# Heads ordered by weight norms, first squares beside the casts, one store per part of Q and K, operand rows loaded ahead of the shift row, last four projections inside the score loop

## The reference

```python
q = (xn @ Wq) * mod; k = (xn @ Wk) * mod; v = (xn @ Wv) * mod     # mod: cos(phase) * amplitude, per head and dim
scores = einsum('bhid,bhjd->bhij', q, k) / sqrt(D)
scores = scores * cos(2 pi (i - j) / S)
w = softmax(scores); w = (w + roll(w, 1)) / sqrt(2)
attn = einsum('bhij,bhjd->bhid', w, v) @ Wo
# experts: 8 logits per token from xn @ wqkv.T, top 2, softmax over the two
ffn = sum over the two experts e: score * ((silu(a) * g) @ w2[e].T), with a, g = split(xn @ w1[e].T)
out = x + attn + ffn
```

## Time and profile before

| | us |
|---|---|
| median of 3 runs | 681.27 (680.93 to 682.08) |
| the profiled execution's own time | 681.02 |
| its span | 679.1 |
| first score matmul starts | 49.67 |
| PE busy in the span | 595.2 (88%) |
| ACT busy in the span | 524.2 (77%) |

### The profile page before, as it was taken

How to read it: one execution, slowest core, us unless ns; L and a number is a source line. 1 busy time by engine, 2 the same in 40 slices (tenths; PEclk the granted TensorE clock), 3 DMA queues, 4 the chain that set the end, 5 groups by cost and what they waited for, 6 DMA issues and landing times.

```text
span 679.1 us, 11462 instructions
## 1 busy us (share of the span) xinstructions
PE 595.2 (88%) x4181; PEld 209.4 (31%) x4181; DVE 199.2 (29%) x491; ACT 524.2 (77%) x489; POOL 81.7 (12%) x94
## 2 busy tenths in 40 slices
PE   2887766389999999999999999999999998888985
PEld 1341111013333334333333333333333331211213
DVE  6675511002123232323333232332323220000233
ACT  2649945398888788887887888888878889999992
POOL 4100176500000000000000000000000003455000
PEclk9997787599999999999999999999999999999999
DMA  8345122404322224132131322223222100111002
GB/s 236 117 131 171 42 65 67 134 22 130 115 77 82 84 76 117 52 106 68 58 117 60 100 75 84 82 60 99 83 77 82 44 9 21 36 33 34 9 1 65
DMA packets 42813, 52.99 MB, mean 78 GB/s; under 512 B 7245, under 2 KB 32359, under 8 KB 42499
## 3 DMA queue, kind: packets, MB, share of 16 engines
q1 hardware_dynamic: 39616, 47.71, 23.4%
q0 software_dynamic: 2048, 4.20, 2.1%
q10 hardware_dynamic: 1090, 0.30, 0.3%
HBM read 38.54 MB, written 13.63 MB: 77 GB/s over the span
## 4 chain that ended last, share of the span: by engine, by line
PE 58%; ACT 18%; issue 15%; another core or an unknown queue 3%; DVE 2%; DMA 1%; ACTq 1%; SPq 0%; DVEq 0%
PE ps L1270 25%; PE ps L1253 16%; ACT big L652 15%; PE ps L1189 7%; PE ps L1198 5%; ACT cs L644 2%; PE ps L1087 2%; PE ps L1277 1%; PE ps L1287 1%; ACTq L578 1%; PE ps L1179 1%; PE ps L1228 1%; DMA ang<-L_attn_quantum_amplitude 1%; PE ps L1075 1%
## 5 line engine op out<-in xcount | busy, mean ns | idle before, releaser
L652 ACT ACTIVATE big<-ps 128x1536 f32<-128x1536 f32 (+1 forms) x410 | 482.0, 1245 | 114.3 <-PE ps L1253 89.8
L1270 PE MATMUL ps<-big,vh 128*32 128x512 f32 x2048 | 269.5, 616 | 0.0
L1253 PE MATMUL ps<-qa,ka 49*128 49x512 f16 x896 | 164.9, 395 | 52.0 <-ACT big L652 42.0
L1253 PEld LDWEIGHTS ps<-qa,ka 49*128 49x128 f16 x896 | 39.3, 94 | 256.2 <-ACT big L652 221.2
L1189 PE MATMUL ps<-xgT,store 128*128 128x128 f32 (+1 forms) x468 | 72.5, 291 | 0.0
L961 DVE TENSOR_REDUCE m<-ps 128x1 f32<-128x512 f32 x64 | 44.3, 692 | 94.0 <-PE ps L1287 94.0
L1270 PEld LDWEIGHTS ps<-big,vh 128*32 128x32 f32 x2048 | 45.6, 109 | 75.3 <-issue 60.5
L1189 PEld LDWEIGHTS ps<-xgT,store 128*128 128x128 f32 (+1 forms) x468 | 55.7, 181 | 28.2 <-issue 28.2
L532 POOL COPY vh<-vaug 128x144 f32 x16 | 5.1, 319 | 433.8 <-PE ps L1270 407.6
L908 DVE SCALAR_TENSOR_TENSOR cs<-cs,ps 128x384 f32<-128x384 f32 x39 | 21.6, 554 | 75.0 <-ACT cs L644 75.0
L901 DVE COPY xgT<-ps 128x128 f32<-128x128 f32 x39 | 11.4, 292 | 92.0 <-PE ps L1179 92.0
(11 more groups left out here) (164 smaller groups left out, 231.8 us busy)
## 6 DMA issues: line engine op xcount, KB each, us to landing
store<-in_L_ffn_w SPq DMA_DIRECT2D x39, 352.0 KB, 3.0
store<-in_L_ffn_w SPq DMA_DIRECT2D x39, 192.0 KB, 3.1
qk_parts<-store SPq DMA_DIRECT2D x16, 256.0 KB
qa<-qk_parts SPq DMA_DIRECT2D x27, 128.0 KB
slots_x<-vh SPq DMA_DIRECT2D x5, 512.0 KB, 6.2
cs<-slots_x SPq DMA_DIRECT2D x20, 128.0 KB, 3.1
slots_y<-y SPq DMA_DIRECT2D x19, 128.0 KB, 3.1
ka<-qk_parts SPq DMA_DIRECT2D x31, 64.0 KB, 2.2
```

What stands on the lines that cost most here:

```text
L652: nc.scalar.activation(probs[:, prob_of(tiles[0]):prob_of(tiles[-1]) + 1, :], ps[:, bank_of(tiles[0]):bank_of(tiles[-1]) + 1, :], ACT.Exp, ...
L1253: ins = nc.tensor.matmul(ps[:, bank_of(n), :], k[at:at + KQ, P * o:P * o + P], q[at:at + KQ, CW * c:CW * c + CW], start=True, stop=True, t ...
L1270: ins = nc.tensor.matmul(ps[32 * c:32 * c + 32, O_BANKS[p % 2], :], vh[:, p % 2, o + 8 * b, :], probs[:, prob_of(n), :], start=k == 0, sto ...
```

## The change

- `qk_parts` is laid out as [which, part, cos or sin, head, dim, token] instead of [which, head, part, row, token]. A part of a set is stored with one DMA of all 128 partitions (4 DMAs for the first two sets instead of 8, and 4 instead of 8 for the last two). The high parts are stored as soon as they are cast; the remainder of set 0 is made on POOL.
- ACT squares sets 0 and 1 straight behind their casts, into memory of their own.
- The heads are ranked by weights: mod to the fourth times the squared column norms of Wq and of Wk, summed by head. POOL squares the weights, PE sums them (`column_norms`, `sum_by_head`), DVE multiplies. `turn_large`, `peaks`, `turn_peaks` and `take_row` go.
- SP and ACT load head 0's 16- and 32-row groups before the shift rows are stored; both shift rows are loaded by SP after that.
- Chunks 12 to 15 (keys of heads 8 to 15) are projected in rounds 10 to 13, in banks 7 and 5; both second sets are cast and subtracted by DVE in rounds 15 and 17; their squares stand in rounds 19 and 20 instead of 4 and 5, the second eight heads' sums in round 22 instead of 9.
- PE's 16 value matmuls stand in blocks between the projections.

```diff
...
-SECOND_AT = 9
+SECOND_AT = 22
...
-SQUARES_AT = (4, 5)
+LATE_AT = 10
+PARTS_AT = (15, 17)
+SQUARES_AT = (19, 20)
...
-PROJ_BANKS = (2, 3, 0, 1)
+PROJ_BANKS = (2, 3, 0, 1, 2, 3, 0, 1, 2, 3, 0, 1, 7, 5, 7, 5)
...
-    scratch = nc.dram_tensor("qk_parts", [2, H, 2, ROWS, S], F16, kind="Internal").ap()
...
+    scratch = nc.dram_tensor("qk_parts", [2, 2, 2, H, D, S], F16, kind="Internal").ap()
...
         def load_operands(eng, h, q, k, half, loaded):
-            def one(ap):
-                return ap.rearrange("o a r n -> (o a r) n")
+            def rows(which, parts_of, n):
+                return scratch[which, parts_of, :, bass.ds(h, 1), :, n].rearrange("a b o d n -> (a b) (o d) n")
...
+            every, cols = slice(0, S), slice(HALF * half, HALF * half + HALF)
+            eng.dma_start(q[at + 1:at + 1 + ROWS, :], rows(0, slice(0, 1), every)).then_inc(loaded, 16)
+            eng.dma_start(q[at + 1 + ROWS:at + KQ, :], rows(0, slice(0, 2), every)).then_inc(loaded, 16)
+            eng.dma_start(k[at + 1:at + 1 + 2 * ROWS, :], rows(1, slice(0, 2), cols)).then_inc(loaded, 16)
+            eng.dma_start(k[at + 1 + 2 * ROWS:at + KQ, :], rows(1, slice(0, 1), cols)).then_inc(loaded, 16)
...
-            def store_parts(i):
-                sp.wait_ge(parts_ready, i + 1)
+            def store_part(i, part):
+                if part == 0:
+                    sp.wait_ge(hi_ready, i + 1)
+                elif i == 0:
+                    sp.wait_ge(first_rest, 1)
+                else:
+                    sp.wait_ge(parts_ready, i)
...
-                for part in range(2):
-                    for half in range(2):
-                        sp.dma_start(scratch[which, 8 * g:8 * g + 8, part, 8 * half:8 * half + 8, :],
-                                     parts[64 * half:64 * half + 64, i, part, :]).then_inc(scratch_wr, 16)
-            def load_head(p, halves=(0, 1)):
+                sp.dma_start(scratch[which, part, :, 8 * g:8 * g + 8, :, :].rearrange("b h d n -> b (h d) n"),
+                             parts[:, i, part, :]).then_inc(scratch_wr, 16)
+            def load_shift(p, h, half):
+                sp.dma_start(qa[p % 2][64 * half:64 * half + 1, :], shift_rows[bass.ds(h, 1), :]).then_inc(aug_ld[p % 2], 16)
+            def load_head(p):
...
-            store_parts(0)
-            store_parts(1)
+            store_part(0, 0)
+            store_part(1, 0)
+            store_part(0, 1)
+            store_part(1, 1)
+            sp.wait_ge(scratch_wr, 4 * 16)
+            sp.wait_ge(rows_ready, 1)
+            sp.wait_ge(order_ready, 1)
+            h = sp.value_load(head_order[0:1, 0:1], min_val=0, max_val=H - 1)
+            load_operands(sp, h, qa[0], ka[:, 0, :], 0, aug_ld[0])
...
-            sp.wait_ge(scratch_wr, 8 * 16)
-            sp.wait_ge(rows_ready, 1)
-            load_head(0, (0,))
+            sp.wait_ge(shift_wr, 16)
+            for half in range(2):
+                load_shift(0, h, half)
...
                     if r == -(-issued // 2):
...
+                if r - 1 in PARTS_AT:
+                    for part in range(2):
+                        store_part(2 + PARTS_AT.index(r - 1), part)
                 if r == SECOND_AT + 3:
...
+            pool.wait_ge(wmat_ld, 4 * 16)
+            nc.gpsimd.tensor_tensor(squared_w[:], wmat[:, 0:2, :], wmat[:, 0:2, :], ALU.mult).then_inc(squared_ready, 1)
...
+            pool.wait_ge(hi_ready, 1)
+            nc.gpsimd.tensor_tensor(parts[:, 0, 1, :], rotated[0], parts[:, 0, 0, :], ALU.subtract).then_inc(first_rest, 1)
...
             def square(i):
-                act.wait_ge(parts_ready, i + 1)
+                if i < 2:
+                    act.wait_ge(hi_ready, i + 1)
+                else:
+                    act.wait_ge(parts_ready, i)
...
+            square(0)
...
+            square(1)
...
-            square(0)
...
-            square(1)
+            other_of(0)
+            nc.scalar.activation(warm[:], ident[:, 0:1], ACT.Exp)
+            act.wait_ge(order_ready, 1)
+            act.wait_ge(scratch_wr, 4 * 16)
+            act.wait_ge(rows_ready, 1)
+            h = act.value_load(head_order[0:1, 0:1], min_val=0, max_val=H - 1)
+            load_operands(act, h, qa[0], ka[:, 0, :], 1, aug_ld[0])
...
-            other_of(0)
-            nc.scalar.activation(warm[:], ident[:, 0:1], ACT.Exp)
-            high_part(2)
-            act.wait_ge(order_ready, 1)
-            act.wait_ge(scratch_wr, 8 * 16)
-            act.wait_ge(rows_ready, 1)
-            act.wait_ge(shift_wr, 16)
-            h = act.value_load(head_order[0:1, 0:1], min_val=0, max_val=H - 1)
-            load_operands(act, h, qa[0], ka[:, 0, :], 1, aug_ld[0])
-            act.dma_start(qa[0][64:65, :], shift_rows[bass.ds(h, 1), :]).then_inc(aug_ld[0], 16)
-            high_part(3)
...
             def rest(i):
+                if i >= 2:
+                    nc.vector.tensor_copy(parts[:, i, 0, :], rotated[i]).then_inc(hi_ready, 1)
...
+            def reach_of_heads():
+                dve.wait_ge(norms_ps, 1)
+                then(nc.vector.tensor_tensor(reach[:, 0:1], mod[:, 2:3], mod[:, 2:3], ALU.mult))
+                then(nc.vector.tensor_tensor(reach[:, 1:2], reach[:, 0:1], reach[:, 0:1], ALU.mult))
+                then(nc.vector.tensor_scalar(reach[:, 0:1], ps[:, SIDE_BANK, 0:1], reach[:, 1:2], None, ALU.mult))
+                nc.vector.tensor_tensor(reach[:, 2:3], reach[:, 0:1], ps[:, SIDE_BANK, 1:2], ALU.mult).then_inc(reach_ready, 1)
+            def take_reach():
+                dve.wait_ge(reach_ps, 1)
+                then(nc.vector.tensor_copy(rank[:, 0, :], ps[0:1, SIDE_BANK, 2:2 + H]))
...
-                if n == 5:
-                    rest(0)
+                if n == 1:
+                    reach_of_heads()
+                if n == 3:
+                    take_reach()
+            order_first()
...
+            mean_squares(0)
...
-            mean_squares(0)
...
+            shifts(0)
...
-            peaks(0)
-            shifts(0)
-            order_first()
-            for n in range(12, 16):
-                rotate(n)
-            rest(2)
-            rest(3)
...
                 if r == RANK_AT:
...
+                if LATE_AT <= r < LATE_AT + 4:
+                    dve.wait_ge(rot_ready, 12 + r - LATE_AT)
+                    rotate(12 + r - LATE_AT)
+                if r in PARTS_AT:
+                    dve.wait_ge(rot_ready, 16)
+                    rest(2 + PARTS_AT.index(r))
                 if r == EXPERTS_AT - 1:
...
+                elif n < 12:
+                    pe.wait_ge(rot_ready, n - 3)
...
+                    pe.wait_ge(rot_ready, max(n - 1, 12))
+                    pe.wait_ge(slot_ready, 1)
...
+            def column_norms():
+                pe.wait_ge(squared_ready, 1)
+                pe.wait_ge(ones_ready, ONES)
+                for which in range(2):
+                    ins = nc.tensor.matmul(ps[:, SIDE_BANK, which:which + 1], squared_w[:, which, :], ones[:, 0:1], start=True, stop=True)
+                ins.then_inc(norms_ps, 1)
+            def sum_by_head():
+                pe.wait_ge(reach_ready, 1)
+                pe.wait_ge(head_ld, 3 * 16)
+                nc.tensor.matmul(ps[0:1, SIDE_BANK, 2:2 + H], reach[:, 2:3], of_head[:], start=True, stop=True).then_inc(reach_ps, 1)
...
+            column_norms()
...
-            for n in range(4, 12):
+            sum_by_head()
+            for n in range(4, 8):
...
-                values(2 * n - 8)
-                values(2 * n - 7)
+            for t in range(8):
+                values(t)
+            rotate(8)
+            rotate(9)
+            rotate(10)
...
-            rotate(12)
-            turn_large(0)
+            for t in range(8, 12):
+                values(t)
...
-            rotate(13)
-            turn_peaks(0)
-            rotate(14)
-            rotate(15)
+            rotate(11)
+            for t in range(12, NT):
+                values(t)
...
+                if k == 0 and p == 1:
+                    pe.wait_ge(rot_ready, 16)
...
-            pe.wait_ge(rot_ready, 16)
+            pe.wait_ge(rot_ready, 12)
...
+                if LATE_AT <= r < LATE_AT + 4:
+                    rotate(12 + r - LATE_AT)
                 if r == SECOND_AT:
...
-                if r == SECOND_AT + 1:
-                    turn_large(1)
                 if r == SECOND_AT + 2:
...
-                if r == SECOND_AT + 3:
-                    turn_peaks(1)
```

72 lines of the change are left out of this document (22 added, 50 removed).

## The result

The changed kernel takes 716.58 us (median of 4 runs, 715.31 to 717.73) against 681.56 for the kernel before in the same series (680.93 to 682.08): ratio 1.0514, 95% interval 1.0493 to 1.0535. It is 35 us slower. 720 was predicted. The profiled execution took 716.17, its span is 714.4.

The account below looks back on a forecast made before the run. It took PE to bound the loop and the chain of waits to bound the prologue, with stores confined to 2 DMA engines; 34.9 + 3 + 1 = 38.9 on 681.0 gave 720 us, likeliest case 710 to 744, 8 in 10 for 703 to 754.

Parts of the forecast that it names:

- The spread rule: Scratch stores and loads: the DRAM access's outermost count sets the engines used, so whole-partition stores run on 2 of 16.
- Step 1: Prologue stores of sets 0 and 1: 512 packets on 2 engines take 43.5 us from 27.0, all in DRAM at 70.5.
- Step 2: Head 0's loads, then shift store and shift loads: first score matmul at 84.6, 34.9 us later than before.
- Step 3: Stores of the last two sets, in the loop, delay the first expert weights: PE waits 3 us (0 to 12).
- Step 4: Projections moved into loop rounds 10 to 13, two groups of 1.08 on PE, partly hidden: +1 us (0 to 2).
- The sum: Whole kernel: 34.9 + 3 + 1 = 38.9 us added to the profiled 681.0, giving 720 us.
- Sixteen engines: Rival on the prologue stores: whole-partition stores use all 16 engines, loop starts 5.5 us earlier, 676.5 us; chance 9%.
- eight engines: Rival on the prologue stores: the spread stays at 8, loop starts 0.9 us earlier, 681 us; chance 3%.
- the first rival: Rival on the prologue stores: whole-partition stores use all 16 engines, stores end at 35.0, 676.5 us; chance 9%.
- The two engines in the loop: Rival: head loads, expert weights and token tiles queue on the same two engines; 2 us per head, 748 us; chance 8%.
- The second pass: Rival on the head order by weights: a head outside the exact ones leaves range, second pass runs, over 1000 us; under 1%.
- remark on the waits without a releaser: Loop rounds 10 to 13: 24.2 us of waits for ACT or unseen releases between 49.6 and 130 hide some added work.

Follow-up runs that it names:

- e1: The changed kernel with each whole-partition store cut into two stores of 64 rows, outermost count 64 instead of 2: 676.96 us, 0.997 of the kernel before.
- e2: The changed kernel with the scratch layout, stores and loads of the kernel before, its other edits kept: 673.05 us, 0.992 of the kernel before.
- e3: The kernel before with only the change's scratch layout, whole-partition stores and new loads: 715.43 us, 1.055 of the kernel before.
- e4: The changed kernel with stores split into 64 rows and head loads cut to outermost count 8, 12 DMAs a head instead of 8: 679.80 us, ratio 1.001.
- e6: e2 with GpSimd's 32 indirect scatters replaced by 32 plain SyncE DMAs in token order, result wrong: 657.29 us, 0.965 of the kernel before.
- e5: e2 with head 0's shift store and shift loads moved ahead of the wait for the stores and the operand loads: 671.39 us, 0.985 of the kernel before.

## Why the prediction was right

**The spread rule** (outermost count sets the number of DMA engines) was read from two shares, 0.48 and 0.89, and extended to 2 blocks, which no row showed. It held: 0.127, 51 GB/s against 0.12 and 48. e1 shows it with bytes and layout fixed, e2 with the partitions of e1's stores. The Trainium skill's rule (DMA: Bandwidth & Descriptors, "Why a DMA increments its semaphore by 16 and not by 1") gives 8, 2 and 16 engines for these patterns, and the shares 0.485, 0.127 and 0.9 agree. What the same page says for one transfer of 128 partitions in place of two halves (the Trainium skill, DMA: Bandwidth & Descriptors, section "Rules for kernel authors") would have spoken for the changed stores; e3 measures 1.055 for them. The prediction left out another row of that same table of the Trainium skill, by which an outermost dimension below 16 confines a DMA to at most that many engines: that row, and not the one on halves, fits the 0.127.

**Step 1** was 2.7 us too long: stores landed at 67.80, predicted 70.5. The term at fault is the packet, 0.157 us for 0.17 (256 x 0.013 = 3.3); the first issue was at 24.91, 0.3 later than predicted, and counted back from the landing the packets begin 0.6 later. A small DVE operation beside POOL's subtraction, 2.54 us instead of 0.21 (below), helped to move the last part from 31 to 33.6; it queued behind the others all the same.

**Step 2**, from the parts' landing to the first score: 14.1 predicted and 14.1 measured (67.80 to 81.89). That is partly luck: from the first load issue to the shift rows in DRAM it took 10.8 instead of 10.0, perhaps because a load takes 0.65 to 0.77 to issue, and the shift loads landed faster, 1.58 for 2.6.

**Step 3** was close: stores end 100.2 us into the loop (103.4), first weights issued at 101.3, PE at the first weights 104.9 us in. The prediction named the weights alone; the token rows are issued behind the same stores and made PE wait first, 3.56 us, with 0.57 and 1.55 for weights. Together 5.7 in place of 3, inside its 0 to 12.

**Step 4** was mis-sized. A chunk is one group of 1.08, and there are four of them, not two: 4.3 us of PE work and not 2.2. Against it stand two terms that the prediction hadn't. The hold-up shrank: its pieces on the chain of waits are 23.0 us before and 15.8 after (ACT's waits without a releaser 24.2 and 19.2). And the granted clock moved: from the first score matmul to the first expert rows its mean is 0.82, before 0.77, so that PE's busy time there grew by 1.4 us only (69.0 to 70.4). With the 3.6 of late rows that stretch comes to 3.6 + 1.4 - 7.2 = -2.2; measured are -1.6 (100.7 for 102.3). Behind it the loop is 4.7 longer. By the starts of the expert tiles 3.3 of them are lost up to the fifth tile: the late weights, and PE's work behind the waits at a lower clock (0.78 from 183 to 190 us, 1.00 behind the first expert rows of the kernel before). The other 1.4 stand behind the last tile's start, in e2 too, and have no named cause. Together +3.1, where the prediction has +4.

**The sum.** Start 32.2 (34.9), loop 3.1 (4.0): 35.3 on the spans (38.9). The medians differ by 35.0. That the loop's +3.1 is near the predicted +4 is in part luck: larger terms of both signs cancel, and two of them, the hold-up and the clock, weren't in the prediction.

**The rivals.** Sixteen engines and eight engines are out by the share. (e1, whose stores do use 16, comes to 677, the 676.5 of the first rival, but not by its sum: it starts at 51.0 and not at 44, and its loop is 7 us shorter.) The two engines in the loop: 1.55 us of late weights at 218 us are all that the changed kernel shows of it, though e4 shows that a busier SP queue makes it real. The second pass didn't run. What the prediction got wrong in kind is its remark on the waits without a releaser: it took them as cover that hides some of the added work. They are a loss of their own, which belongs to the scatters: without these the stretch up to the first expert rows is 18 us shorter (e6 against e2).

## What to carry to other kernels

Before a DMA is made "bigger", count the outermost blocks of its DRAM side: a merge that turns 8 blocks into 2 turned some 14 us of stores (27.1 to 41.4) into 43 (24.9 to 67.8), though bytes and row length stayed. Split the transfer so that the outer count is larger (here 16 and 32 rows reached a share of 0.89, 64 rows 0.9), and look at both ends of a scratch tensor, the issue time of the reads too (e4). And where several engines wait together for nothing that the profile names, look at what else is being issued then: on the chips with a hold-up 32 indirect scatters cost 14 to 18 us (e6 against e5 and e2), more than the 6 that the rest of the change wins in e2.

## What the runs showed of the hardware beyond that

- **Indirect scatters hold other engines up.** Loop without them 18 us shorter up to the first expert rows (77.8 against 95.6, e6 and e2). On one of the chips the kernel before was 25 to 27 us faster, and the two kernels profiled there, both paced, had no such wait. What holds the engines, and why not on that chip, is open. POOL's 32 indirect gathers late in the kernel, one per quad, show none.
- **A wait in the full loop costs more than its length.** Behind PE's idle time the granted clock is near the lower of its two levels, 1.2 of 2.4 GHz, for some microseconds: 4.5 us of waiting became 6.4 in e4 (0.59 over 180 to 186 us), where six expert matmuls took 1.65 us and later 0.93.
- **Price of a 4 KB packet**: 0.157 us with 2 engines busy; 0.485 x 16 x 12 / 489 = 0.19 with 8.
- **Issue time depends on the pattern**: the same 16 or 32 rows, 0.32 to 0.40 us on SP from one run of rows, mostly 0.65 to 0.8 from 2, 4 or 8 blocks (head 0's to head 2's loads, ahead of the scatters).
- **DVE beside POOL.** A 64-element DVE operation took 2.54 us while POOL subtracted 128 x 2048 elements, and 0.21 right behind. It ends 0.1 us after POOL does; so it does in e2, where it began 2.9 us ahead of that end, not 2.5, and took 2.94. The 128 x 512 products just ahead of it, in part beside the same subtraction, kept their 0.8 us. Timelines of the changed kernel, DVE and POOL:

```profile
26.59 2.54 DVE L808 TENSOR_TENSOR rank_pairs<-rank 1x64 f32<-1x64 f32 x1
29.16 0.21 DVE L809 TENSOR_TENSOR rank_pairs<-rank 1x64 f32<-1x64 f32 x1
24.96 4.09 POOL L551 TENSOR_TENSOR store<-big,store 128x2048 f16<-128x2048 f32 x1 [1.94 <-ACT store L629]
```
